# A two-layer outer-product network on Trainium2: block input and pieces of the second weights handled earlier in each slot

## The reference

```python
B, M, D = 2048, 39, 16       # x0: r_x, float32
x0 = xk = x
for W in (W0, W1):           # (1, 39*39, 128), (1, 39*128, 128)
    Wr = W.reshape(m, Hk, Hn)
    xk = jnp.einsum('bid,bjd,ijh->bhd', x0, xk, Wr)
    outs.append(xk)
return jnp.sum(jnp.concatenate(outs, axis=1), axis=-1)   # (2048, 256)
```

## Time and profile before

| | us |
|---|---|
| median of 3 runs | 581.03 (580.76 to 582.3) |
| profiled execution | 579.92 |
| its span | 578.1 |

### The profile page before, as it was taken

One profiled execution on the slowest core, in us unless ns is written; L12 is line 12 of the kernel. 1 busy time (PEld: TensorE's weight loads), 2 busy tenths in 40 slices (PEclk: granted clock), 3 DMA queues, 4 the chain that ended last, 5 costly groups with the idle time before them and its releaser, 6 DMA issues.

```text
span 578.1 us, 10856 instructions
## 1 busy us (share of the span) xinstructions
PE 550.1 (95%) x3186; PEld 483.1 (84%) x3186; DVE 472.1 (82%) x816; ACT 470.0 (81%) x983; POOL 480.9 (83%) x407
## 2 busy tenths in 40 slices
PE   5788788999999999999999999999999999999998
PEld 3476677878888888988988998898889889889988
DVE  4688888888888898888889888888988888888740
ACT  4698888889888888888888888888888888888740
POOL 6998899899989888889988888898888899888800
PEclk9799999999999999999999999999999999999999
DMA  8999999999899989999999989999999989988210
GB/s 318 331 352 317 326 312 304 306 305 295 267 306 332 307 298 290 279 324 287 288 301 312 303 268 305 315 296 293 313 285 281 325 292 300 295 304 285 52 52 10
DMA packets 66489, 163.78 MB, mean 283 GB/s; under 512 B 10112, under 2 KB 18816, under 8 KB 66432
## 3 DMA queue, kind: packets, MB, share of 16 engines
q1 hardware_dynamic: 66432, 163.09, 88.0%
HBM read 139.98 MB, written 2.10 MB: 246 GB/s over the span
## 4 chain that ended last, share of the span: by engine, by line
PE 71%; ACT 10%; DMA 6%; issue 5%; POOL 4%; DVE 2%; SPq 1%; ACTq 0%; DVEq 0%; POOLq 0%
PE acc L397 12%; PE acc L399 11%; PE acc L398 11%; PE fin L448 6%; PE fin L449 6%; PE fin L450 6%; DMA outs<-w_dram 5%; PE pg L433 5%; PE pg L431 5%; PE pg L432 5%; ACT fh L510 4%; PE turn L409 4%; PE acc L392 2%; POOL fl L761 2%; ACT gh L552 1%
## 5 line engine op out<-in xcount | busy, mean ns | idle before, releaser
L761 POOL TENSOR_TENSOR fl<-fs,fh 128x512 fp32r<-128x512 f32 x192 | 249.7, 1304 | 42.8 <-ACT fh L510 40.1
L397 PE MATMUL acc<-fh,w0h 128*128 128x512 f32 x384 | 160.3, 417 | 15.3 <-ACT x L533 10.1
L756 POOL TENSOR_TENSOR fs<-xr,xs 128x512 f32<-128x512 f32 x128 | 163.0, 1295 | 0.9 <-DMA xr<-xb_dram 0.8
L647 DVE TENSOR_TENSOR fp<-xl,xr 128x512 f32<-128x512 f32 x192 | 133.5, 697 | 31.4 <-ACT xl L517 18.4
L399 PE MATMUL acc<-fl,w0h 128*128 128x512 f32 x384 | 151.9, 395 | 0.0
L398 PE MATMUL acc<-fh,w0l 128*128 128x512 f32 x384 | 151.5, 395 | 0.0
L651 DVE TENSOR_TENSOR fl<-fp,fh 128x512 fp32r<-128x512 f32 x192 | 131.9, 687 | 23.1 <-ACT fh L510 18.2
L510 ACT ACTIVATE fh<-fp 128x512 fp32r<-128x512 f32 x192 | 114.5, 596 | 36.3 <-PE acc L399 30.6
L666 DVE TENSOR_TENSOR gl<-pg,gh 128x320 fp32r<-128x320 f32 x252 | 117.0, 486 | 25.8 <-ACT gh L552 20.6
L510 ACT ACTIVATE fh<-fs 128x512 fp32r<-128x512 f32 x192 | 121.4, 632 | 10.8 <-PE acc L399 8.6
L552 ACT ACTIVATE gh<-pg 128x320 fp32r<-128x320 f32 x252 | 105.5, 439 | 18.4 <-PE pg L433 17.6
(11 more groups left out here) (67 smaller groups left out, 724.0 us busy)
## 6 DMA issues: line engine op xcount, KB each, us to landing
xr<-xb_dram SPq DMA_DIRECT2D x192, 512.0 KB, 5.7
xbd<-xdhl SPq DMA_DIRECT2D x256, 80.0 KB, 4.0
xs<-xa_dram SPq DMA_DIRECT2D x64, 256.0 KB, 4.1
xdr<-xd_dram SPq DMA_DIRECT2D x64, 160.0 KB, 3.9
xp<-xpairs_dram SPq DMA_DIRECT2D x32, 256.0 KB, 4.3
outs<-w_dram SPq DMA_DIRECT2D x9, 256.0 KB, 6.6
out_dram<-outs SPq DMA_DIRECT2D x7, 256.0 KB, 5.8
fs<-w0a_dram SPq DMA_DIRECT2D x1, 256.0 KB, 4.8
```

The lines of the kernel that those rows point to most:

```text
L397: nc.tensor.matmul(acc[:, :], w0h[:, t, :], fh[:, t, :], start=t == 0, stop=False)
L647: nc.vector.tensor_tensor(f_at(t), xl[:, :], xr[:, gi % 2, t, :], ALU.mult).then_inc(prod_dve, 1)
L756: nc.gpsimd.tensor_tensor(f_at(t), xr[:, gi % 2, t, :], xs[:, gi % 2, :], ALU.mult)\
L761: nc.gpsimd.tensor_tensor(fl[:, t, :], f_at(t), fh[:, t, :], ALU.subtract).then_inc(low_pool, 1)
```

## The change

Four engines' passes are reordered; no instruction is added or removed. On ACT, xd_split goes from behind the turned copy to ahead of high(g+1,0), in every slot but the first, and the piece's high part from there to right behind high(g+1,0). On DVE, the piece's low part goes from behind the turned copy's low part to behind low(g+1,0). On POOL, the low parts of the block input and of the piece go from behind low(g+1,1) to ahead of low(g,5). On SP, the piece's load goes from behind the second and third right-operand loads to ahead of them.

```diff
@@ SP: chunk @@
                     if more2:
                         load_xd(g + 2)
+                    if (first or second) and 0 <= g + 1 - W1_SLOT < PIECES:
+                        w1_load(g + 1 - W1_SLOT)
                     if more3:
                         wait_product(sp, g + 1, 3)
                         load_right(j, gi + 3, 1)
                     if more3:
                         wait_product(sp, g + 1, 5)
                         load_right(j, gi + 3, 2)
-                    if (first or second) and 0 <= g + 1 - W1_SLOT < PIECES:
-                        w1_load(g + 1 - W1_SLOT)
@@ ACT: chunk @@
                         g_high_part(j, gi - 2, 1, was_odd, None)
+                    if more and g:
+                        xd_split(j, gi + 1, False)
                     if more:
                         high(g + 1, 0, False)
+                    if (first or second) and 0 <= g - W1_SLOT < PIECES:
+                        w1_high_part(g - W1_SLOT)
...
                     if prev:
                         turned_high(g - 1)
-                    if more:
-                        xd_split(j, gi + 1, first and gi == 0)
-                    if (first or second) and 0 <= g - W1_SLOT < PIECES:
-                        w1_high_part(g - W1_SLOT)
+                    if first and gi == 0:
+                        xd_split(0, 1, True)
@@ DVE: chunk @@
                         product(j, gi + 1, 2, False)
                         low(g + 1, 0)
+                    if 0 <= g - W1_SLOT < PIECES:
+                        w1_low_part(g - W1_SLOT)
+                    if more:
                         product(j, gi + 1, 3, False)
...
                         turned_low(g - 1)
-                    if 0 <= g - W1_SLOT < PIECES:
-                        w1_low_part(g - W1_SLOT)
@@ POOL: chunk @@
                         product(j, gi + 1, 1, False)
                         product(j, gi + 1, 4, False)
-                    if g:
-                        low(g, 5)
-                    if more:
-                        low(g + 1, 1)
+                    if more and g:
                         xd_split(g + 1, gi + 1)
                     if (first or second) and 0 <= g - W1_SLOT < PIECES:
                         w1_low_part(g - W1_SLOT)
+                    if g:
+                        low(g, 5)
+                    if more:
+                        low(g + 1, 1)
+                    if first and gi == 0:
+                        xd_split(1, 1)
```

More of the change, by code:

```diff
@@ L789, in chunk @@
                         product(j, gi + 1, 4, False)
+                    if more and g:
+                        xd_split(g + 1, gi + 1)
+                    if (first or second) and 0 <= g - W1_SLOT < PIECES:
+                        w1_low_part(g - W1_SLOT)
                     if g:
@@ L793, in chunk @@
                         low(g + 1, 1)
-                        xd_split(g + 1, gi + 1)
-                    if (first or second) and 0 <= g - W1_SLOT < PIECES:
-                        w1_low_part(g - W1_SLOT)
+                    if first and gi == 0:
+                        xd_split(1, 1)
                     if more:
```

## The result

The changed kernel takes 599.23 us in the median of six runs (597.18 to 605.12), against 581.66 us for the kernel before on the same chips: a ratio of 1.0327, 95% interval 1.0266 to 1.0388. The forecast was 586.0 us, in a range from 576.5 to 595.0. The direction was right, the size was 5.0 us where 17.6 were measured, and the time lies above the range. The profiled execution took 597.18 us, with a span of 595.4.

The account below looks back on a forecast made before the run. TensorE was taken to bound the steady part, with ACT's waits costing time earlier. Terms 2.1 (slots 2 to 5) + 2.1 (first slot) - 0.7 (ten piece slots) + 1.5 (steady part) = +5.0 us, giving 586.0 us; range 576.5 to 595.

Parts of the forecast that it names:

- What bounds the kernel: Whole run: TensorE bounds the steady part; slots 6 to 15 at 8.4 us each would win 5.7 us.
- The piece's load: Slots 6 to 15, SP: issued 0.9 us earlier, landing in about 5.3 us, 2.3 us earlier in all; operand loads' delay costs nothing.
- not removed but moved: Slot 9, ACT: the 0.9 us wait for the piece moves to a place with 0.53 us of cover.
- The loop of ACT, SP and the load: Every slot: ACT's early split waits for the block input's load, whose issue hangs on POOL and SP; slots 2 to 5, +2.1 us.
- 12.8 + L: Loop time for two slots with squares; L is the block input load's time from issue to landing.
- That term: Slots 2 to 5: with L = 4.3, 8.5 us a slot against 7.96, so +2.1 us (0 to +5).
- The steady part: 46 of the 64 slots: loop 16.6 against TensorE's 16.8 us for two slots, not binding at the median; +1.5 us (-1 to +8).
- Rival (c): Steady part: the loop binds, 8.6 us a slot with L = 4.2, +9.2 in place of 1.5; 593.7 us, chance 0.13.
- The first slot: Slot 1: ACT's work and POOL's low(1,5) go behind the load's landing, so slot 2 begins +2.1 us late (1.5 to 3).
- POOL's order: Low parts ahead of low(g,5): TensorE stopped for 0.7 us in slots with a piece, nothing in steady slots (up to 0.5).
- The ten slots with a piece: Slots 6 to 15: 8.9 us a slot, 89 in all, -0.7 us (-4.7 to +3.3).
- The rules: Skill pages: in-order queues speak against the early split; the bandwidth page's 2.9 us estimate was set aside for measured landings.

Follow-up runs that it names:

- e3: Kernel before with only the piece's load issued ahead of the two right-operand loads; 577.35 us, ratio 0.9895 to 0.9958.
- e1: Changed kernel with the block input's split left in its old place on ACT and POOL, so only the piece's four moves; 585.3 us.
- e2: Kernel before with only the block input's split moved early on ACT and POOL, the piece wholly as before; 599.46 us.
- e5: Changed kernel with the early split only from slot 16 on, its old place in slots 1 to 15; 595.57 us.
- e9: Changed kernel with the block input's loads left out from group 2 on, splits and block transfers kept; 586.46 us.
- e15: Changed kernel with the block input's load issued last in SP's pass, behind both operand loads; 683.48 us.
- e13: Changed kernel with ACT's split right behind high(g+1,0), ahead of the squares, and POOL's order as before; 590.49 us.
- e8: Changed kernel with POOL's order put back: low(g,5) and low(g+1,1) ahead of the low parts of block input and piece; 599.24 us.
- e4: Changed kernel with the block input's load issued ahead of the four block transfers and the pair on SP; 601.28 us.
- e6: Changed kernel with the early split only in slots 1 to 15, its old place from slot 16 on; 587.32 us.
- e10: Kernel before with the block input's loads left out from group 2 on; 576.59 us.
- e11: Changed kernel with the block input's split in its old place and POOL's order as before, the piece's other moves kept; 586.11 us.
- e7: Changed kernel with the block input's split on ACT right behind high(g+1,0) instead of ahead of it; 601.3 us.

## Why the prediction was wrong

**What bounds the kernel** held: the steady part was TensorE's, with nothing to gain and room to lose; e3 got 5.0 us out of the ten slots with a piece, where 5.7 were said to be in reach.

**The piece's load.** The landing after 5.3 us in place of 6.7 came out in e3, and the cost of nothing for the operand loads behind it. ACT's use of the piece, "not removed but moved", was right too, but it stood in the sum as part of a loop at 8.9 us a slot; in e1 these ten slots took 9.3.

**The loop of ACT, SP and the load.** That the load's landing holds up the early split was right (e2, e5, e9, e15). Its formula, 12.8 + L, looks close. In slots 2 to 5 the changed kernel's loads landed after 3.4 us in the median instead of the 4.3 I took; 12.8 + 3.4 is 8.1 us a slot, and 32.83 / 4 = 8.2 were measured. That term was +2.1 and came out at +1.0. But this is no test of the formula: e1, e3 and e5, with the split in its old place there, took 33.0 to 33.1 us for the same slots, at a granted clock of 0.95. In the steady part the landings were 4.0 us in the median, these being the landings of L279 issued from 29 to 62, and from 160 to 500 us:

```profile
DMA to landing us min/median/max: 2.6/3.4/5.1
...
DMA to landing us min/median/max: 2.7/4.0/6.3
```

**The steady part is the step that failed.** I put +1.5 us on it, since the loop "does not bind at the median", and it cost 11.0. Two things were wrong in this term. The median of the earlier trace rows, 3.6 us, lies just under the 3.8 us at which I had the loop bind, and I priced the term by it, though a lateness is never paid back: TensorE was busy all the time, so only the loads above the mark count, and those below it give nothing in return. The timeline of the changed kernel has ten slots of over 9.0 us after slot 16 where the kernel before has none. The upper bound of 8 us for the term was too low as well: 48 slots at 12.8 + 0.2 + 4.0 = 17.0 for two would be +4.8 us, so a median alone, even the right one, doesn't give the loss. And the way was another: the prediction followed ACT's queue to POOL's next product. The chain, and e13 against e8, show that the load holds up high(g+1,0), with it DVE's whole run up to the turned copy's low part, and so TensorE's pg products, which in turn release SP's next block transfers (the chain enters SP at 256.25, right behind TensorE's products of pg). I had named DVE only for the piece. Rival (c), this mechanism at full strength, gave 593.7 us and 13% of the chance; it should have had the most.

**The first slot.** +2.1 us were forecast, slot 2 near 32.6. It began at 33.88, and at 33.4 to 34.1 us in e2, e4 and e6 to e9, against 30.5 to 31.1 in the kernel before, e1, e5, e10 and e11 (e3, also without it, had 32.7). The split waited as said, and POOL's low(1,5) with it, in the timelines of ACT, POOL and TensorE:

```profile
28.39 0.47 ACT L540 ACTIVATE xdhl<-xdr 128x320 fp32r<-128x320 f32 x1 [4.74 <-DMA xdr<-xd_dram]
...
28.94 0.86 POOL L768 TENSOR_TENSOR xdhl<-xdr,xdhl 128x320 fp32r<-128x320 f32 x1 [2.64 <-ACT xdhl L540]
29.76 3.75 POOL L764 TENSOR_TENSOR fl<-fs,fh 128x512 fp32r<-128x512 f32 x3
...
31.17 0.76 PE L397 MATMUL acc<-fh,w0h 128*128 128x512 f32 x1 [4.00 <-POOL fl L764]
```

The sum misread its own second figure. It said that ACT and POOL both give 2.1 us, but it had POOL's low(1,5) move from 26.02 to 29.5, which is 3.5 us. It started at 29.76, 3.7 us later than before, and TensorE's sixth accumulation with it, at 31.17 in place of 27.45. In the kernel before there was 1.0 us of slack behind it (the three products of tile 5 were done at 28.4, high(2,5) started at 29.43); now high(2,5) waits for them, and behind it come only the copy of the left operand and the copy that opens slot 2:

```profile
32.83 0.63 ACT L510 ACTIVATE fh<-fs 128x512 fp32r<-128x512 f32 x1 [0.98 <-PE acc L399]
```

What the sum left out is TensorE's clock. It fell within those 4.00 us of idle time, and from 30 to 34 us the granted clock is 0.50, 1.2 GHz, where the kernel before had 1.00 (table of busy time by stage, PEclk third from the end):

```profile
30.00:34.00 4.00, 2.83 (x7) 2.09 (x8) 3.27 (x7) 3.02 (x7) 4.00 (x4) 0.50 1.06 336
```

"TensorE: Matmul & The Clock Gate" of the Trainium skill, on what is happening, has the clock halved by idleness, and the row agrees. The three products of tile 5 took 1.6 us, from 31.17 to 32.8, in place of 0.9. So the 3.4 us are 3.7 less 1.0 of slack, and 0.7 from the clock. It was missing from the rivals. The load isn't the only thing that slot 1 waits for, either: e9, without it, begins slot 2 at 33.86, as the split also waits for the block transfers that read its output. The prediction has no term for that buffer.

**POOL's order.** It was costed at up to 0.7 us a slot with a piece. POOL held TensorE up for 9.9 us in nine waits, 4.0 of them in slot 1; undoing it alone (e8) saved nothing, with the split behind high(g+1,0) it saved 10.8 us (e13 against e7). What I had not thought of is that a moved POOL instruction can stretch one of DVE's.

**The ten slots with a piece** came to 91.4 us against the 89 forecast. ACT's wait for the piece nearly went (0.9 us in two waits in the changed kernel, 6.4 before), against what I expected to see; it now waits for the block input ahead of it instead.

**The rules.** The strictly ordered queues of ACT and DVE, from the Trainium skill's "TensorE: Matmul & The Clock Gate", decided here as said: in the slot above high(g+1,0) starts at 264.66, right behind the split that waited. The other estimate, 2.9 us by "DMA: Bandwidth & Descriptors" of the Trainium skill, was rightly set aside as a value of L: the changed kernel's medians for this load are 3.4 to 4.0 us.

**What stays open.** In the changed kernel itself the low part of the squares takes 0.71 us in the median from slot 16 on (up to 1.41), so there its loss is mostly by late loads, and e9 leaves 1.8 us of 11.0 for all else. Why e8, with yet longer waits for the load, ends at the same time as the changed kernel was not taken apart. And TensorE's clock was not separated from the waits before slot 16. In slots 2 to 15 the changed kernel's granted clock is 0.96, where the kernel before has 1.00; by these rows, an estimate, that is 0.04 of 124.3 us, or 5 us of full clock, more than the 2.8 us lost there. e6 and e8 have 36 us in slots 2 to 5 at a clock of 0.91 and 0.90, where the changed kernel has 32.8 at 0.96. What makes the clock fall in one execution and not in the next, with the same code, is open, and the small terms ahead of slot 16 are sizes of single executions.

## What to carry to other kernels

A step that waits for a transfer may move ahead in an in-order queue only as far as the landing allows in the slowest case, counted from what releases its issue; every buffer that the step writes has a landing of its own to check. Where one engine is busy all the time, price a new wait by how often its data is late and by how much, not by the median, for early data pays nothing back. Issue order is the cheaper tool: putting the late load ahead of loads with three slots to spare won 0.7% (e3), and using it earlier as well lost that and more (e1). Two kernels that differ only behind a stretch can still differ in it by the clock, so its granted clock is read beside its length.

## What the runs showed of the hardware

DVE's subtraction of 64x512 elements with both operands in SBUF took 0.69 us alone and 1.54 us beside a POOL subtraction of 128x512 (e7, 23 of 23 times). DVE's instructions with one operand in PSUM kept 0.68 to 0.70 us beside POOL (e7). What stretches it looks like a wait for the whole POOL instruction and not like a shared rate: DVE's subtraction of 128x256 elements in e8 took 0.42, 0.71, 1.02 and 1.25 us where the POOL subtraction that was under way ended 0.13, 0.43, 0.74 and 0.96 us after DVE's start (109.25, 91.36, 72.74 and 100.43), so each time 0.28 to 0.29 us after POOL's end. Where no POOL instruction ran, it took 0.42 us (83.18 and 127.54).

One load of 160 KB, issued at the same place of each slot, took from 2.7 to 6.3 us to land in the steady part of the changed kernel, at a DMA share of 0.87. Issued ahead of the block transfers (e4) it took no less, 3.1 to 6.5 us with a median of 4.5, though 320 KB fewer were queued between the start of SP's pass and it.
